# Attention by pairs of groups on two halves of the partitions, with reordered transposes, maxima and copies

## What is computed

```python
y = clip(einsum('blc,oc->blo', x * styles, weight) * dcoefs + bias, -256, 256)
Q = (y @ Wq).reshape(n, s, 4, 4, 64)        # 4 groups, 4 heads each, width 64
K, V = (y @ Wk), (y @ Wv)                   # 4 groups, width 64
raw = einsum('bsgwe,btge->bstgw', Q, K * 64 ** -0.5)
A = einsum('bstgw,btge->bsgwe', softmax(raw, axis=2), V)
x = x + y + A.reshape(n, s, 1024) @ Wpost
kx = modulated_linear(x, cond, ...)         # then heads of width 8 within a token
out = modulated_linear(softmax(kx kx^T / sqrt(8)) kx, cond, ...)
x = x + moe(out)                            # top 2 of 8 experts, experts over capacity dropped
```

## Time and profile before

| | |
|---|---|
| median of 3 runs | 661.29 us |
| the profiled execution | 660.68 us |
| its span, first to last instruction | 658.9 us |
| PE matmuls busy | 622.5 us, 94% |
| PE weight loads | 506.5 us, 77% |
| DVE | 521.1 us, 79% |
| ACT | 413.2 us, 63% |
| POOL | 288.1 us, 44% |
| HBM traffic | 6.9 MB, 11 GB/s over the span |

### The profile page before, as it was taken

One profiled execution on the slowest core, in us unless ns is written; L12 is line 12 of the kernel. 1 busy time (PEld: TensorE's weight loads), 2 busy tenths in 40 slices (PEclk: granted clock), 3 DMA queues, 4 the chain that ended last, 5 costly groups with the idle time before them and its releaser, 6 DMA issues. The chain is left out here.

```text
span 658.9 us, 15267 instructions
## 1 busy us (share of the span) xinstructions
PE 622.5 (94%) x4388; PEld 506.5 (77%) x4420; DVE 521.1 (79%) x1155; ACT 413.2 (63%) x823; POOL 288.1 (44%) x251
## 2 busy tenths in 40 slices
PE   8899999999999999999999999999999996889998
PEld 8687778787878787878787878787878786756665
DVE  6246888888888888888888888888888879877766
ACT  2776767777676767777777777777777541334343
POOL 5122555555555555555555555555555457000000
PEclk9999999999999999999999999999999999899999
DMA  7200000000000000000000000000000000000004
GB/s 244 50 1 1 1 2 1 0 0 0 0 0 0 0 0 0 0 0 0 0 0 0 0 0 0 0 0 0 0 0 1 2 0 1 1 0 1 0 0 127
DMA packets 9364, 7.18 MB, mean 11 GB/s; under 512 B 1089, under 2 KB 8833, under 8 KB 9217
## 3 DMA queue, kind: packets, MB, share of 16 engines
q1 hardware_dynamic: 9344, 6.94, 3.6%
HBM read 4.84 MB, written 2.10 MB: 11 GB/s over the span
## 5 line engine op out<-in xcount | busy, mean ns | idle before, releaser
L1092 POOL TENSOR_TENSOR pair<-kx 128x1152 f32<-128x1152 f32 x32 | 82.4, 2574 | 164.1 <-ACT kx L836 159.8
L611 PEld LDWEIGHTS bank_a<-v,prob 128*128 128x128 f32 x1024 | 127.0, 192 | 17.0 <-issue 15.8
L603 PE MATMUL bank_t<-qT,k_one 128*128 128x512 f32 x256 | 130.7, 592 | 6.1 <-POOL neg_diag L1084 4.7
L611 PE MATMUL bank_a<-v,prob 128*128 128x65 f32 x1024 | 131.8, 272 | 0.0
L295 DVE TENSOR_REDUCE row_max<-bank_s 128x4 f32<-128x512 f32 x128 | 87.3, 682 | 13.3 <-PE bank_s L594 8.9
L836 ACT ACTIVATE prob<-bank_t 128x512 f32<-128x512 f32 x128 | 76.3, 596 | 29.6 <-PE bank_t L603 26.4
L440 DVE CAST k<-k_one 64x512 bf16<-64x512 f32 x32 | 50.1, 1565 | 54.3 <-ACT k_one L836 54.3
L1072 POOL TENSOR_TENSOR mix_hi<-mix_hi 128x512 f32<-128x512 f32 (+2 forms) x96 | 80.2, 835 | 7.5
L1084 POOL TENSOR_TENSOR neg_diag<-neg_max,own_w 16x512 bf16<-16x512 f32 x32 | 36.3, 1135 | 95.9 <-ACT neg_max L836 83.1
L836 ACT ACTIVATE qT<-misc 64x512 f32<-64x512 f32 x128 | 75.5, 590 | 4.0 <-PE misc L618 1.6
L618 PEld LDWEIGHTS misc<-yT,wq_sb 128*128 128x128 f32 x512 | 64.5, 192 | 15.9 <-issue 14.9
(11 more groups left out here) (155 smaller groups left out, 1103.3 us busy)
## 6 DMA issues: line engine op xcount, KB each, us to landing
out<-acc_all SPq DMA_DIRECT2D x8, 256.0 KB, 2.3
x_all<-in_xT SPq DMA_DIRECT2D x1, 1024.0 KB, 9.0
w_sb<-in_w SPq DMA_DIRECT2D x2, 512.0 KB
x_all<-in_xT SPq DMA_DIRECT2D x1, 768.0 KB, 6.9
wq_sb<-in_wq SPq DMA_DIRECT2D x1, 512.0 KB, 4.5
wpost_sb<-in_wpost SPq DMA_DIRECT2D x1, 512.0 KB, 9.8
x_all<-in_xT SPq DMA_DIRECT2D x1, 256.0 KB, 3.6
b_rows<-in_b SPq DMA_DIRECT2D x16, 4.0 KB
```

What stands on the lines that cost most here:

```text
L603: mm(bank_t[g % 2][:, :, :], k_one[:, j, g, :], qT[:, j, HPG * g:HPG * (g + 1), :], start=False, stop=True).then_inc(s_t_mm, 1)
L611: last = mm(att_bank(g)[:, w, :], prob[:, g % 2, w, :], v1[:, j, g, :], start=(w == 0), stop=True, skip_group_check=True)
L1092: G.tensor_tensor(pair[:, :, :], bass.AP(kx2, jc * 2 * P, [[4 * P, P], [0, SHIFTS], [1, P]]), bass.AP(kx2, jc * 2 * P, [[4 * P, P], [MD, S ...
```

## The change

The heads are regrouped on the host (Wq's columns) so that a block of 128 columns holds one head of an even and one of an odd group. Queries and keys of even groups then lie on partitions 0 to 63, those of odd groups on 64 to 127, without zero rows: qT, q16, kT, k16 are indexed by pair. `scores` multiplies 64 rows. `scores_t` works on a pair: two bias products of 64 rows into the two banks bank_t, then four fp32 products of 256 columns, in turn from the lower and the upper half. row_max becomes bf16 and gets its maxima on a diagonal; four bf16 products with an identity put them, transposed and already spread, into bank_s, and one ACT copy with factor -1 writes neg_diag (128x512) from there, without GpSimd. ACT copies queries and keys over all 128 partitions and casts the keys too, from PSUM. y_raw goes to PSUM (misc[0]), where the clamp on DVE reads it. GpSimd does the residual add. misc banks have fixed uses, each with its wait, and bank_free goes.

PE's order in a slot after: queries 0, att transpose 1, scores 3, queries 1, products of the maxima, Wpost, scores_t pair 0, keys and values, kx, attend 0, attend 1, kx transpose, y product, mix transpose, scores_t pair 1, scores 0 (of sample a), output product, attend 2, scores 1, attend 3, att transpose 0 (of sample s), scores 2. The filling products keep_going and the gate's products keep their slots.

```diff
...
-        k16 = sb("k16", [P, 2, GROUPS, P], BF16)
+        qT = sb("qT", [P, 2, PAIRS, HPG, P])
+        q16 = sb("q16", [P, 2, PAIRS, HPG, P], BF16)
+        kT = sb("kT", [P, 2, PAIRS, P])
+        k16 = sb("k16", [P, 2, PAIRS, P], BF16)
         v1 = sb("v1", [P, 2, GROUPS, KEY + 1])
-        row_max = sb("row_max", [P, P])
-        neg_max = sb("neg_max", [P, P])
...
-                V.tensor_reduce(row_max[:, KEY + HPG * g:KEY + HPG * (g + 1)], bank_s[:, :, :], AX.X,
-                                ALU.max).then_inc(s_max, 1)
+                V.tensor_reduce(bass.AP(row_max, max_row(g), [[HPG * P, P], [P + 1, HPG]]).unsqueeze(2),
+                                bank_s[:, :, :], AX.X, ALU.max).then_inc(s_max, 1)
...
-                if A:
-                    dve.wait_ge(s_k, 2 * n(a))
-                    need(dve, s_s_mm, 4 * n(a - 2))
-                    V.tensor_copy(k16[0:KEY, ja, :, :], k_one[0:KEY, ja, :, :]).then_inc(s_k16, 1)
...
                 if has(a + 1):
                     dve.wait_ge(s_y_raw, n(a + 1))
                     need(dve, s_kv_mm, n(a))
                     need(dve, s_xy, n(a))
-                    V.tensor_scalar(yT[:, :], y_raw[:, :], CLAMP, -CLAMP, ALU.min, ALU.max).then_inc(s_yT, 1)
+                    V.tensor_scalar(yT[:, :], misc[0][:, 1, :], CLAMP, -CLAMP, ALU.min, ALU.max).then_inc(s_yT, 1)
+                if A:
+                    group_max(a, 0)
+                    group_max(a, 1)
+                if B:
+                    invert(s, 2)
+                    normalise(s, 2)
+                    invert(s, 3)
+                    normalise(s, 3)
+                if A:
+                    group_max(a, 2)
...
                 need(pe, s_max, 4 * s + g)
+                if g == 0:
+                    need(pe, s_neg, s)
                 pe.wait_ge(s_q16, 2 * s + g // 2 + 1)
+                rows = slice(KEY * (g % 2), KEY * (g % 2 + 1))
                 for w in range(HPG):
-                    last = mm(bank_s[:, w, :], q16[:, j, HPG * g + w, :], k16[:, j, g, :],
+                    last = mm(bank_s[:, w, :], q16[rows, j, g // 2, w, :], k16[rows, j, g // 2, :],
                               start=(w == 0), stop=True, skip_group_check=True)
                 last.then_inc(s_s_mm, 1)
-            def scores_t(s, j, g):
-                need(pe, s_prob, 4 * s + g - 1)
-                pe.wait_ge(s_own, n(s))
-                mm(bank_t[g % 2][:, :, :], g_rows[:, g, :], neg_diag[:, j, :, :], start=True, stop=False)
-                mm(bank_t[g % 2][:, :, :], k_one[:, j, g, :], qT[:, j, HPG * g:HPG * (g + 1), :],
-                   start=False, stop=True).then_inc(s_t_mm, 1)
+            def scores_t(s, j, p):
+                need(pe, s_prob, 4 * s + 2 * p)
+                pe.wait_ge(s_neg, n(s))
+                for half in range(2):
+                    rows = slice(KEY * half, KEY * (half + 1))
+                    mm(bank_t[half][:, :, :], g_rows[rows, 2 * p + half, :], neg_diag[rows, j, :, :],
+                       start=True, stop=True, skip_group_check=True)
+                for w in range(0, HPG, 2):
+                    for half in range(2):
+                        rows = slice(KEY * half, KEY * (half + 1))
+                        last = mm(bank_t[half][:, w:w + 2, :], kT[rows, j, p, :], qT[rows, j, p, w:w + 2, :],
+                                  start=False, stop=True, skip_group_check=True)
+                        if w == HPG - 2:
+                            last.then_inc(s_t_mm, 1)
...
+                if A:
+                    pe.wait_ge(s_yT, n(a))
+                    queries(a, 0)
                 if C:
-                    bank_free(pe, 1, s, "att0")
-                    att_transpose(c, 0)
+                    need(pe, s_x1T, c)
+                    if has(d - 1):
+                        pe.wait_ge(s_tok, d)
+                    att_transpose(c, 1)
                 if B:
                     scores(s, j, 3)
...
+                if A:
+                    if C:
+                        pe.wait_ge(s_attT, 2 * c + 1)
+                    need(pe, s_q, 2 * a)
+                    queries(a, 1)
+                if B:
                     pe.wait_ge(s_max, 4 * s + 4)
-                    nc.tensor.transpose(misc[1][:, 0, :], row_max[:, :], ident[:, :]).then_inc(s_neg_mm, 1)
-                if s_is(s, BATCH - 1):
-                    gate_logits(parts_early[0])
+                    for w in range(HPG):
+                        last = mm(bank_s[:, w, :], row_max[:, w, :], ident16[:, :],
+                                  start=(w == 0), stop=True, skip_group_check=True)
+                    last.then_inc(s_neg_mm, 1)
...
                 if B:
                     scores_t(s, j, 0)
                 if A:
-                    if not s_is(a, 0):
-                        bank_free(pe, 0, s, "q1")
-                    queries(a, 1)
...
-                if s_is(s, BATCH):
-                    gate_logits(parts_early[4])
-                if B:
-                    scores_t(s, j, 1)
-                if C:
-                    pe.wait_ge(s_kxT, n(c))
-                    nc.tensor.transpose(misc[1][:, 0, :], kxT[:, :], ident[:, :]).then_inc(s_kxn_mm, 1)
...
+                    pe.wait_ge(s_q, 2 * a + 1)
+                    bank = misc[0]
                     for i in range(2):
                         mm(bank[:, i, :], wk_sb[:, i * P:(i + 1) * P], yT[:, :],
                            start=(i == 0), stop=True, skip_group_check=True)
                     mm(bank[:, 2:4, :].rearrange("p a f -> p (a f)"), yT[:, :], wv_sb[:, :], start=False,
                        stop=True, skip_group_check=True).then_inc(s_kv_mm, 1)
-                if late(s):
...
+                if C:
+                    if A:
+                        pe.wait_ge(s_q, 2 * a + 2)
+                    pe.wait_ge(s_x1s, n(c))
+                    mm(misc[1][:, 0, :], modw_sb[:, 1, :], x1s[:, :], start=True, stop=True).then_inc(s_kx_mm, 1)
...
+                if B:
+                    attend(s, j, 0)
...
+                if B:
+                    attend(s, j, 1)
+                if C:
+                    pe.wait_ge(s_kxT, n(c))
+                    nc.tensor.transpose(misc[1][:, 0, :], kxT[:, :], ident[:, :]).then_inc(s_kxn_mm, 1)
+                if has(a + 1):
+                    if A:
+                        pe.wait_ge(s_v, n(a))
+                        pe.wait_ge(s_k16, n(a))
+                    pe.wait_ge(s_xs, n(a + 1))
+                    mm(misc[0][:, 0, :], modw_sb[:, 0, :], xs[:, j, :], start=True, stop=True).then_inc(s_y_mm, 1)
...
-                    bank_free(pe, 1, s, "o")
-                    pe.wait_ge(s_mixT, n(d))
-                    mm(misc[1][:, 0, :], modw_sb[:, 2, :], mixT[:, :], start=True, stop=True).then_inc(s_o_mm, 1)
...
+                    if C:
+                        pe.wait_ge(s_x1T, n(c))
...
+                    need(pe, s_tok, d)
+                    pe.wait_ge(s_mix, n(d))
+                    nc.tensor.transpose(misc[2][:, 0, :], mix[:, :], ident[:, :]).then_inc(s_mixT_mm, 1)
...
+                if B:
+                    scores_t(s, j, 1)
...
+                if D:
+                    pe.wait_ge(s_mixT, n(d))
+                    mm(misc[2][:, 0, :], modw_sb[:, 2, :], mixT[:, :], start=True, stop=True).then_inc(s_o_mm, 1)
+                if B:
+                    attend(s, j, 2)
...
                 if B:
-                    attend(s, j, 2)
+                    attend(s, j, 3)
+                if B:
+                    if A:
+                        pe.wait_ge(s_q, 2 * a + 2)
+                    if C:
+                        pe.wait_ge(s_kx2, n(c))
+                    att_transpose(s, 0)
                 if A:
                     scores(a, ja, 2)
-                if B:
-                    attend(s, j, 3)
-                if has(a + 1):
-                    bank_free(pe, 0, s, "y")
-                    pe.wait_ge(s_xs, n(a + 1))
-                    mm(misc[0][:, 0, :], modw_sb[:, 0, :], xs[:, j, :], start=True, stop=True).then_inc(s_y_mm, 1)
...
-                for par in range(2):
-                    f(qT[0:KEY, j, HEADS // 2 * half + par:HEADS // 2 * (half + 1):2, :],
-                      qkv_bank(b, ("q0", "q1")[half])[par * KEY:(par + 1) * KEY, :, :]).then_inc(s_q, 1)
+                f(qT[:, j, half, :, :], misc[half][:, :, :]).then_inc(s_q, 1)
...
-                heads = slice(HEADS // 2 * half, HEADS // 2 * (half + 1))
-                f(q16[0:KEY, j, heads, :], qT[0:KEY, j, heads, :]).then_inc(s_q16, 1)
+                f(q16[:, j, half, :, :], qT[:, j, half, :, :]).then_inc(s_q16, 1)
...
                     copy_att(c, 0)
+                if A:
+                    copy_q(a, ja, 0)
+                if C:
                     copy_att(c, 1)
+                if A:
+                    narrow_q(a, ja, 0)
                 if B:
                     act.wait_ge(s_neg_mm, n(s))
-                    need(act, s_own, n(s - 1))
```

(47 more changed lines are left out.)

182 lines of the change are left out of this document (55 added, 127 removed).

## The result

The changed kernel takes 620.64 us (619.27 to 621.60), where the kernel before took 661.18 in the same comparison; the ratio is 0.9385 [0.937, 0.940]. That is 40.5 us less. The prediction of 636 had the sign and the range of 608 to 664 right, and the gain 15 us too small; the time lies 1.4 us under the 622 to 648 of its likeliest case. The profiled execution took 620.5 us.

What follows compares the result with a forecast made beforehand. TensorE's stream was taken as the bound. The terms summed to -0.81 us a slot, x31 = -25.1, so 660.7 became 635.6, with 0.6 added for the median 636.2 us; range 608 to 664.

Steps and rivals of the forecast that it cites:

- The pair: Transposed scores on TensorE: two groups overlap wholly on the two row halves, 4.28 to 2.14 us a slot.
- Switches: TensorE changing between 64-row and 128-row products: ten a slot, 0.15 us in and 0.20 out, +1.75 us a slot.
- Waits of before: TensorE waits that go, us a slot: keys' cast -0.45, GpSimd's step for the maxima -0.15, scores 2's maximum -0.13.
- The new wait: TensorE waits ahead of attend 2, as a pair's exponentials start only when the whole pair is done: +0.20 us a slot.
- Edits off the stream: Changes on ACT, DVE and GpSimd, including the clamp's PSUM source and GpSimd's add: slack, no time.
- The next edge: ACT's copies of v and keys come ahead of the y product by less than 1 us, the next to be late.
- The signs: Maxima's products every 15.3 us, halves starting within 0.01, pair 1.07, 0.15 to 0.20 lost per stay side, DVE under 80%.
- A: Rival: TensorE switches cost only 0.09 us each, 0.9 instead of 1.75 a slot, 610 us; chance 0.12.
- B: Rival: TensorE begins passes strictly in program order, so a pair takes five steps, +0.43 us a slot, 650 us; chance 0.12.
- C: Rival: 64-row bf16 weights load at the fp32 rate and switches cost 0.20, +0.32 us a slot, 671 us; chance 0.08.
- D: Rival: the two row halves of the transposed scores don't overlap, +1.33 us a slot, 702 us; chance 0.05.
- E: Rival: another wait takes over (v and keys on ACT, DVE's chain), 0.5 to 0.9 us a slot, 652 to 664; chance 0.10.

Runs made afterwards that it cites:

- experiment 8: Kernel after with the residual add back on DVE and the clamp reading y_raw in SBUF again: 669.26 us, ratio 1.0132.
- experiment 9: Kernel after with only the clamp's source back in SBUF (y_raw), the residual add staying on GpSimd: 670.40 us, ratio 1.0101.
- experiment 11: Kernel after with the clamp reading y_raw in SBUF, written as a scalar_tensor_tensor instead of a tensor_scalar: 687.58 us, ratio 1.0404.
- experiment 7: Kernel after without 64-row products in the slots (keys zero-padded, transposed scores group by group), y product moved just ahead of attend 2: 643.97 us, ratio 0.9740.
- experiment 4: Kernel after with bf16 scores on 128 zero-padded rows, y product just ahead of attend 2, its ACT copy and clamp later: 594.73 us, ratio 0.8995.
- experiment 5: Kernel after, all 64-row stays kept, with only the y product moved to just ahead of attend 2: 613.28 us, ratio 0.9280.
- experiment 6: Kernel before with only the keys' bf16 cast moved from DVE to ACT: 648.78 us, ratio 0.9813.
- experiment 10: Kernel after with only the residual add moved from GpSimd to DVE, the clamp still reading PSUM: 621.03 us, ratio 0.9383.
- experiment 2: Kernel after with bf16 scores on 128 rows, keys zero-padded per group by two ACT copies, pairs kept: 606.53 us, ratio 0.9183.
- experiment 3: Kernel after's order and copies without 64-row products in the slots: keys of both precisions zero-padded, transposed scores group by group: 662.57 us, ratio 1.0014.
- experiment 1: Kernel after with each half's fp32 product as one of 512 columns instead of two alternating ones of 256: 620.71 us, ratio 0.9383.

## Why the prediction was right, and its size wrong

**The bound.** Right. TensorE's stream set the slot before and after, and each experiment moved the time through it, experiments 8, 9 and 11 by waits and a lower clock.

**The pair.** Predicted 2.14 us, measured 2 x 1.08 against 4.28: 2.12. Experiment 7 against 4 confirms it net of its switches. The maxima's four products take the 0.22 that was taken for them (320.16 to 320.39).

**Switches.** This is the term that was mis-sized. Predicted 0.15 in, 0.20 out, 1.75 a slot. The slot's rows show 0.10 in five times, and out 0.19 three times and 0.14 to 0.19 twice: 1.35 to 1.45 in sum. I had priced the way in from fp32 weights on both sides and taken off only a part of it. But even these are too much for the sum, because the kernel before lost something behind its 128-row scores too. What a 64-row stay costs over its 128-row form is 3 x 0.19 for the scores (experiment 5 against 4) and 4 x 0.14 for the pairs (7 against 4): 1.12 a slot. The term was too large by 0.63 a slot, 20 us, which is more than the whole miss of 0.55 a slot.

**Waits of before.** The cast's 0.45 was right (experiment 6). The three that I counted make 0.73. Experiment 7 has the new order and copies without any 64-row product, and its slot is 0.55 shorter than the one before, with 0.11 more for the maxima in it: the waits that went are 0.66, 0.74 if its own idle 0.08 is added. Right.

**The new wait.** Predicted 0.20 ahead of attend 2; L734 to L588 is 0.53 for two passes (0.22) and the rest of a switch (0.05 to 0.10), so 0.21 to 0.26, and experiment 5, which fills it, is 0.21 a slot faster. Right.

**The sum.** With these sizes it is -2.14 + 0.11 + 1.12 - 0.66 + 0.21 = -1.36 a slot, and 1.36 was measured. It closes because the terms are differences between the slots of five kernels in a row (before, 7, 4, 5, after); how each splits into switch and wait is still argued from rows.

**Edits off the stream.** "These give slack, no time" is the step that failed in its reason. That it did not spoil the number is luck, since the edit was in the change: by experiments 9 and 10 the PSUM source of the clamp is worth 49 us. The kernel before clamps from SBUF too, but hardly ever beside GpSimd: two of its 32 clamps begin before an add of GpSimd's has ended, by 0.2 us, and take 0.33. Its instructions (duration in ns, min/median/max):

```profile
L467 DVE TENSOR_SCALAR yT<-y_raw x32: 226/228/326, 13.7 to 507.0; 128x128 f32<-128x128 f32 x32
```

The change moves the clamp into the pair product. I asked what the clamp would wait for, and not what it would meet. The row that could have warned was at hand: the keys' cast of 1565 ns in a kernel where such a cast should be short. DVE's timeline of the kernel before shows the same collision:

```profile
322.53 1.63 DVE L440 CAST k<-k_one 64x512 bf16<-64x512 f32 x1 [1.12 <-ACT k_one L836]
```

With POOL's timeline beside it:

```profile
321.32 2.56 POOL L1092 TENSOR_TENSOR pair<-kx 128x1152 f32<-128x1152 f32 x1 [5.13 <-ACT kx L836]
```

It ends at 324.16, 0.28 behind the product's end at 323.88. The two of 32 casts that begin while GpSimd is idle take 0.42, and the other 30 begin inside the pair product and end 0.25 to 0.28 behind it. With 0.42 this one would have ended at 322.95, ahead of the attend that ends at 323.85. So by these rows the 0.45 us of "scores 0 wait for the cast" was this lock too; no run moves the cast away from the product on DVE to show it.

**The next edge.** Predicted: v and keys ahead of the y product, by less than 1 us. Right, and it bit twice (experiments 2 and 3).

**The signs.** The pair, the halves' common start, DVE under 80% (75) and the clock of 1.00 in the loop came as said; the products of the maxima recur every 14.72 us and not 15.3, and the way into a stay loses 0.10 and not 0.15.

**The rivals.** A (switches at 0.09, 610 us) had the better price: 1.12 for ten switches is 0.11 each, although its way out loses up to 0.19 in the rows. The time lies 11 us from it and 15 from the forecast. B is refuted by experiment 1, C by the scores' own starts (four of 64 rows begin within 0.17 us of each other, at 318.85 and up to 319.02, and L595 at 319.17), D by the pair. E did not happen in the kernel after, but one source operand stood between it and 670 us.

## What to carry to other kernels

Price a moved instruction by what runs beside it in its new place, for DVE on GpSimd and the other way round, and not only by its own length; a row several times as long as its shortest instance is likely a collision, and it tells which operand to move to PSUM. A 64-row pair of fp32 products pays here (1.58 us a slot net of its switches), while the single 64-row stays of short bf16 products cost 0.19 us each and are better written on 128 padded rows, provided that the padding's copies have slack. When a part is undone for a test, look in the trace for the wait that the undoing itself brought, before the number is believed.

## What the runs showed of the hardware that I had not expected

A DVE clamp of an SBUF tile beside a GpSimd instruction went from 0.23 or 0.29 to a median of 1.46 or 1.53 us, with one SBUF input or with two, while the same clamp from PSUM took 0.29. Waits of 0.5 to 0.7 us in TensorE's stream cost as much again through the clock, 24 us against 23 in experiment 8 and 32 against 23 in experiment 9, and nothing through it in experiment 3. And two halves of the array's rows keep their own chains of fp32 passes in both orders of the program (experiment 1).
